# A fused patch embedding, top-k attention and routed FFN on one core: GpSimd's, TensorE's and ScalarE's orders rewritten, three row counts moved from ScalarE to VectorE

## The chip, the cores and the metric

The kernel runs on one core of one Trainium2 chip, as one program. The metric is the device time of an execution in microseconds; three executions of the kernel before gave 3077.92 (median), 3074.23 and 3079.49. An execution that the hardware profiler recorded took 3077.82 us, of which 3076.1 us are the span from the first to the last instruction.

## The reference

For 64 batches, 36 image patches and a class token are embedded (a 768 to 256 projection and a layer norm), and 128 text tokens are put behind them: T = 165 tokens of width 256. Then, in float32:

```
h = h + attention(layernorm(h))     # 16 heads of width 16; of each row of 165 scores
                                    # only the largest int(165*0.3) = 49 are kept
h = h + moe(layernorm(h))           # 64 experts of width 192, top 8 per token, capacity 128,
                                    # and one shared expert
```

Attention is `softmax` over the 49 kept scores of each row times `v`, and an output projection. There are 16*165 = 2640 score rows in a batch.

## The kernel before, in words

The work falls into two phases. In the first one, a loop over the batches (`batches`, unrolled, 68 iterations) does everything but the routed experts; in the second one, `experts` gathers rows for each expert. The change touches the first only.

One batch passes through several iterations, so that iteration i works on five of them at once. For batch i+1 it makes the front: norm, transposition, q, k and v (`front_*`) and the first score tiles. For batch i it makes scores and exponentials, and counts. For batch i-1 it selects the 49 values and masks. For batch i-2 it transposes the probabilities and multiplies by v (`transposes`, `transposed`, `values`), and projects. For batch i-3 it does the second norm, the shared expert and the routing (`back_*`). For batch i-4 GpSimd writes token numbers into a table in HBM by indirect DMAs (`back_slots` for text, 8 per batch; `packed` for image tokens, 8 per three batches: three in each of two iterations and two in the third). Every third iteration also embeds the patches of three batches (`trio(i+4)`: `front_embed*` on VectorE, `front_scale` and `front_affine` on GpSimd).

The 2640 rows are 21 tiles of 128 rows, in 7 groups of 3 tiles. TensorE makes a group's scores in one of three PSUM banks (`scores`), VectorE copies them to S and takes the row minima `nb` (`take`, L1083), ScalarE makes exponentials E and their sums `sz` (`exps`, L865). Selection searches a threshold per row. GpSimd guesses it from `nb` and `sz` (`guess`, half 0 is tiles 0 to 8, half 1 is tiles 9 to 20). ScalarE counts the values above the guess (`count` with n = 0, L877), GpSimd corrects it (`refine`), ScalarE counts again (n = 1), GpSimd corrects once more (`refine2`). GpSimd then writes X = (S + threshold) * 2^-40, a group at a time, into five rotating buffers (`apart`, L662). A third count is taken of X: by ScalarE for groups 0, 1, 2 (`third_count`, L890) and by VectorE for groups 3 to 6 (L1096). From it VectorE knows how far the count is off 49 and to which side (`side`, `side2`, for sets of groups: {0,1,2}, {3,4}, {5,6}), flips the signs by a bitwise xor (`one_side`, L1148), lists the eight nearest values (`nearest`, L1158, which frees the X buffer), ranks, and masks E into PR (`mask`, L1277).

Each engine runs its list `iteration(i, r)` strictly in the order in which it is written, and waits on semaphores that others raise. No planner or cost stands behind the order: it is written out by hand. GpSimd raises `s_up` 20 times per batch, and the waits name positions in that sequence. S and E have two buffers each, PTT and PTI (the transposed probabilities) one. ScalarE's copy of v into VZ (`front_v`, L853) and its copies of transposed quads (`transposed`, L901 to L906) free the PSUM banks for TensorE's next step. On the way back, GpSimd's `back_scale` (L651, L653) gives the norm's factor `brs` to VectorE's `back_norm`; TensorE transposes (L1757), ScalarE copies (X2T, L917), TensorE makes both halves of the shared expert (`back_glu`, L1766), ScalarE takes tanh (L921), and VectorE goes on (`back_glu`, L1320).

Of the kernel before, what the change touches and what calls it, by code (L numbers as in the profile page):

```python
# [60 lines left out]
RING = 4  # L61
# [9 lines left out]
def early_fusion_kernel(nc, patches, txt, w_tok, b_tok, cls, pos, gamma, beta, w_qkv, b_q, b_k, b_v, w_out, b_out,  # L71
# [3 lines left out]
    with ctx:  # L75
# [184 lines left out]
        THIRD = [3, 4, 5, 6]  # L260
# [3 lines left out]
        SETS = [(0, 1, 2), (3, 4), (5, 6)]  # L264
# [238 lines left out]
        def _(pool):  # L503
# [107 lines left out]
            def guess(i, r, half):  # L611

                lo, hi = HALVES[half]
                n = UP * i + 5 * half
                pool.wait_ge(s_exp, EX_N * i + hi)
                gated()
                pool.tensor_scalar(v0[:, lo:hi], nb[:, lo:hi], -GUESS[3], GUESS[1], ALU.mult, ALU.add).then_inc(s_up, 1)
                pool.tensor_scalar(v1[:, lo:hi], nb[:, lo:hi], -GUESS[2], GUESS[0], ALU.mult, ALU.add).then_inc(s_up, 1)
                pool.wait_ge(s_up, n + 1)
# [6 lines left out]
            def refine(i, r, half):  # L626
# [6 lines left out]
                pool.wait_ge(s_up, UP * i + 11 + 2 * half)  # L633
# [53 lines left out]
            def pack_tokens(n):  # L687
                if n >= 2:
                    pool.wait_ge(s_packed[n % 2], PS * (n // 2))
# [28 lines left out]
            def iteration(i, r):  # L718
# [8 lines left out]
                if has(i - 1):  # L727
                    apart(i - 1, (r - 1) % RING, 2)
                    apart(i - 1, (r - 1) % RING, 3)
                    apart(i - 1, (r - 1) % RING, 4)  # L730
                if has(i + 1):
                    front_bias(i + 1, (r + 1) % RING)
                if has(i):
                    guess(i, r, 0)
                if has(i - 1):
                    apart(i - 1, (r - 1) % RING, 5)
                if trio(i + 4):
                    front_scale((i + 4) // PACKED)
                if has(i - 1):
                    apart(i - 1, (r - 1) % RING, 6)  # L740
                if has(i - 4):
                    back_tokens(i - 4, r)
                if True:
                    packed(i, 0)
                    packed(i, 1)
                if has(i - 4):
                    back_slots(i - 4, r, 0, 2)
                if True:
                    packed(i, 2)
                if has(i):  # L750
                    guess(i, r, 1)
                if has(i - 4):
                    back_slots(i - 4, r, 2, 4)
                if has(i + 1):
                    front_center(i + 1)
                if has(i):
                    refine(i, r, 0)
                if has(i - 4):
                    back_slots(i - 4, r, 4, 6)
                if has(i):  # L760
                    refine(i, r, 1)
                if has(i - 4):
                    back_slots(i - 4, r, 6, 8)
                if trio(i + 4):
                    front_affine((i + 4) // PACKED)
                if has(i):
                    refine2(i, r, 0)
# [49 lines left out]
        def _(act):  # L817
# [38 lines left out]
            def exps(i, r, g):  # L856

                if g == 0:

                    ahead(act, s_up, UP * (i - 1) + 10, i - 1 if known(i) else i)  # L860
# [7 lines left out]
            def count(i, r, n, tiles):  # L868

                for t in tiles:  # L870
                    if t in (0, AHEAD):
                        half = t // AHEAD
                        act.wait_ge(s_up, UP * i + (5 + 5 * half, 12 + 2 * half)[n])
# [1067 lines left out]
```

## Time and profile before

| | us |
|---|---|
| three executions: median, lowest, highest | 3077.92, 3074.23, 3079.49 |
| the profiled execution, its span | 3077.82, 3076.1 |
| busy: TensorE matmuls, VectorE, ScalarE, GpSimd | 2360.4, 2486.5, 2480.2, 2181.0 |
| granted TensorE clock, mean over the span | 0.88 |

Busy is the time in which an engine ran an instruction other than register, branch, semaphore and DMA-issuing ones. The span holds both phases, so the share of busy time over all of it is lower than in the loop: in the last 350 us the engines other than TensorE do little. Rows of a timeline give the start (us from the span's start), how long the row took, the engine, the line of the kernel, the operation, what it writes and reads, and how many instructions are merged; in brackets the idle time before them, and what ended it.

### The profile page before, as it was taken

What the parts mean: (1) busy time and instruction counts of PE and PEld (TensorE: products, weight loads), DVE (VectorE), ACT (ScalarE), POOL (GpSimd) and SP (SyncE); (2) the same over time, 40 slices, a digit from 0 to 9 for tenths busy, and PEclk for the clock granted to TensorE, in tenths of its full rate; (3) what the DMA queues carried; (4) which work ended last, traced back from release to release, by engine and by line L of the source; (5) the groups of instructions that cost most, each with busy time, mean ns of one, the idle gap of its engine ahead of it and who ended that gap; (6) DMA issues with size and microseconds to landing.
All of it is one profiled execution on the core that took longest, in us unless ns stands there. A gap on an engine that the chain in (4) does not pass through costs nothing.

```text
span 3076.1 us, 74618 instructions
## 1 busy us (share of the span) xinstructions
PE 2360.4 (77%) x17233; PEld 2007.1 (65%) x17233; DVE 2486.5 (81%) x12929; ACT 2480.2 (81%) x11201; POOL 2181.0 (71%) x4319
## 2 busy tenths in 40 slices
PE   5677877778787778777887787787878787764887
PEld 4566666666676666666666676676667676544776
DVE  1798889888888899988989888988899888842444
ACT  3999999999999999989999899998999989811111
POOL 3457777777777777777777777777777777645665
PEclk7799988988999989988899889988888889867998
DMA  2011011010110110101101101001010100006886
GB/s 66 10 30 24 25 27 29 25 30 23 28 25 23 29 30 25 30 23 24 27 25 29 30 25 27 25 22 28 25 30 23 29 18 24 19 16 159 220 222 143
DMA packets 203389, 130.07 MB, mean 42 GB/s; under 512 B 101776, under 2 KB 194444, under 8 KB 202924
## 3 DMA queue, kind: packets, MB, share of 16 engines
q1 hardware_dynamic: 168064, 105.38, 12.7%
q0 software_dynamic: 34368, 19.34, 3.9%
q14 instruction: 333, 2.73, 0.3%
q8 instruction: 132, 2.16, 0.3%
q10 hardware_dynamic: 492, 0.45, 0.1%
HBM read 77.63 MB, written 34.09 MB: 36 GB/s over the span
## 4 chain that ended last, share of the span: by engine, by line
ACT 47%; PE 14%; POOL 13%; issue 11%; DVE 6%; DMA 4%; another core or an unknown queue 2%; ACTq 0%; POOLq 0%; SPq 0%; DVEq 0%
ACT JK L877 23%; ACT E L865 9%; PE bank L1766 4%; ACT PTT L901 4%; DMA out<-E,X 3%; ACT JL L890 3%; POOL slot_token L683 3%; ACT PTI L906 2%; PE bank L1688 2%; PE bank L1691 2%; POOL X L662 2%; POOL out L793 2%; ACT KT L843 1%; PE bank L1757 1%
## 5 line engine op out<-in xcount | busy, mean ns | idle before, releaser
L877 ACT ACTIVATE JK<-S,thr 128x165 f32<-128x165 f32 x2688 | 1120.5, 422 | 14.5 <-POOL thr L624 7.2
L683 POOL DMA_INDIRECT slot_token<-TOKI,SLOT x512 | 533.5, 1042 | 221.8 <-issue 204.4
L662 POOL TENSOR_SCALAR X<-S,nt 128x165 f32<-128x165 f32 x1344 | 582.7, 452 | 75.4 <-DVE LIST L1158 66.1
L865 ACT ACTIVATE E<-bank,nb 128x165 f32<-128x165 f32 x1344 | 508.5, 391 | 10.8 <-DVE S L1083 9.6
L877 ACT ACTIVATION_READ_ACCUMULATOR JK<-S,thr 128x1 f32 x2688 | 510.7, 190 | 0.0
L1277 DVE SCALAR_TENSOR_TENSOR PR<-S,TV,E 128x165 f32<-128x165 f32 x1344 | 480.1, 405 | 0.2
L1083 DVE TENSOR_SCALAR_CACHE_REDUCE S<-bank 128x165 f32<-128x165 f32 x1344 | 364.5, 320 | 86.9 <-PE bank L1691 47.4
L1705 PE MATMUL bank<-IDENT,PR 128*128 128x128 f32 x1344 | 222.2, 283 | 230.3 <-issue 116.1
L1158 DVE MAX8 LIST<-X 128x8 f32<-128x165 f32 x1344 | 351.3, 317 | 8.1 <-DVE X L1148 1.8
L1705 PEld LDWEIGHTS bank<-IDENT,PR 128*128 128x128 f32 x1344 | 154.8, 145 | 284.6 <-issue 163.2
L1688 PE MATMUL bank<-KZ,QA 128*128 128x165 f32 x1408 | 280.8, 346 | 45.6 <-ACT E L865 19.0
L1739 PE MATMUL bank<-PTT,VZ 128*32 128x165 f32 x2048 | 196.4, 432 | 149.9 <-ACT PTT L903 119.9
L1148 DVE TENSOR_TENSOR X<-X,flip 128x495 int32<-128x495 int32 x448 | 295.9, 662 | 0.0
L1688 PEld LDWEIGHTS bank<-KZ,QA 128*128 128x128 f32 x1408 | 231.6, 213 | 79.7 <-issue 73.0
L865 ACT ACTIVATION_READ_ACCUMULATOR E<-bank,nb 128x1 f32 x1344 | 271.7, 202 | 0.0
L1691 PE MATMUL bank<-KZ,QB 128*128 128x165 f32 x1408 | 267.9, 329 | 0.0
L706 POOL DMA_INDIRECT slot_token<-PACKI,PACK x176 | 193.9, 1102 | 81.2 <-issue 64.1
L890 ACT ACTIVATE JL<-X,tiny 128x165 f32<-128x165 f32 x576 | 241.2, 429 | 1.9 <-POOL X L662 1.9
L1691 PEld LDWEIGHTS bank<-KZ,QB 128*128 128x128 f32 x1408 | 233.8, 211 | 0.0
L1739 PEld LDWEIGHTS bank<-PTT,VZ 128*32 128x32 f32 x2048 | 98.3, 151 | 186.3 <-ACT PTT L903 134.7
L1096 DVE TENSOR_SCALAR_CACHE_REDUCE JD<-X 128x165 f32<-128x165 f32 x768 | 205.9, 316 | 3.2 <-issue 1.6
L1766 PE MATMUL bank<-X2T,WSG 128*96 128x165 f32 x1024 | 207.1, 370 | 1.6 <-ACT X2T L917 1.6
(211 smaller groups left out, 6358.3 us busy)
## 6 DMA issues: line engine op xcount, KB each, us to landing
S<-in_w_gate SPq DMA_DIRECT2D x64, 192.0 KB
S<-in_w_up SPq DMA_DIRECT2D x64, 192.0 KB
E<-in_w_down SPq DMA_DIRECT2D x64, 192.0 KB
RD<-inverses SPq DMA_DIRECT2D x128, 82.5 KB
x_rows<-X SPq DMA_DIRECT2D x64, 160.0 KB
H<-in_txt SPq DMA_DIRECT2D x64, 128.0 KB
QA<-QT SPq DMA_DIRECT2D x512, 10.3 KB
QB<-QT SPq DMA_DIRECT2D x512, 10.3 KB
```

What stands on the lines that cost most here:

```text
L662: last = pool.tensor_scalar(X[n % DEEP][:, t % GROUP, :], S[r % 2][:, t, :], nt[r % 2][:, t:t + 1], DOWN, ALU.add, ALU.mult)
L683: pool.indirect_dma_start(slot_token, bass.IndirectOffsetOnAxis(SLOT[r % 2][:, 0, k:k + 1], 0), TOKI[r % 2][:, :], None, bounds_check=SLOT ...
L865: act.activation(E[r % 2][:, t, :], chunks(bS[g % 3], GROUP, T)[:, t % GROUP, :], ACT.Exp, bias=nb[:, t:t + 1], scale=-1.0, accum_out=sz[: ...
L877: act.activation(JK[:, t % 4, :], S[r % 2][:, t, :], ACT.Sign, bias=(t0, t1)[n][:, t:t + 1], scale=-1.0, accum_out=(c0, c1)[n][:, t:t + 1] ...
L890: act.activation(JL[:, n % 3, :], X[(NG * i + g) % DEEP][:, k, :], ACT.Sign, bias=tiny[:, :], scale=-1.0, accum_out=c2[:, t:t + 1]).then_i ...
L1083: dve.tensor_scalar(S[r % 2][:, t, :], chunks(bS[g % 3], GROUP, T)[:, t % GROUP, :], 1.0, None, ALU.mult, ALU.min, accum_out=nb[:, t:t + 1 ...
L1158: dve.max(LIST[:, 0, WIN * t:WIN * t + WIN], X[n % DEEP][:, t % GROUP, :]).then_inc(s_list, 1)
L1277: dve.scalar_tensor_tensor(PR[:, t, :], S[r % 2][:, t, :], TV[:, t:t + 1], E[r % 2][:, t, :], ALU.is_le, ALU.mult, accum_out=den[:, t:t + ...
L1688: last = pe.matmul(o, QA[:, P * t:P * t + P], KZ[:, 0, :], start=True, stop=(t < MIXED))
L1691: last = pe.matmul(o, QB[:, at:at + P], KZ[:, 1, :], start=(t > MIXED), stop=True)
L1705: pe.transpose(bT[:, P * k:P * k + P], PR[:, t, IMG:T], IDENT[:, :])
L1766: last = pe.matmul(chunks(bank, NF, T)[0:FC, f, :], WSG[:, k, at:at + FC], X2T[:, k, :], start=(k == 0), stop=(k == KC - 1))
```

## The change

GpSimd: `guess` is cut in two. Its first two operations, which need `nb` only, wait for `take` (`s_take`); the three that need the exponentials' sums stay behind the wait for ScalarE (`guess2`). The order of the list is new: `front_scale` of a trio goes up between `apart` 2 and 3, `packed(i, 0)` goes ahead of `apart` 5, `front_affine` goes up behind `apart` 6, `front_center` and `refine` of half 0 go ahead of the guess of half 1, and fewer indirect DMAs stand ahead of that guess, more behind it; `refine2` of half 0 goes ahead of the last two. ScalarE: the third count of group 2 is gone, and `front_v` stands ahead of `transposed` 4. VectorE: group 2 is in `THIRD`, the sets are {0,1}, {2,3,4}, {5,6}, `take` 3 goes behind the shared expert and `front_norm2`, and `front_embed2` goes up. TensorE: `back_glu` goes ahead of `scores` 3, `front_v` ahead of `transposes` 4.

```diff
-        THIRD = [3, 4, 5, 6]
+        THIRD = [2, 3, 4, 5, 6]
-        SETS = [(0, 1, 2), (3, 4), (5, 6)]
+        SETS = [(0, 1), (2, 3, 4), (5, 6)]
...
             def guess(i, r, half):
                 lo, hi = HALVES[half]
-                n = UP * i + 5 * half
-                pool.wait_ge(s_exp, EX_N * i + hi)
+                pool.wait_ge(s_take, NT * i + hi)
                 gated()
                 pool.tensor_scalar(v0[:, lo:hi], ...)
                 pool.tensor_scalar(v1[:, lo:hi], ...)
+
+            def guess2(i, r, half):
+                lo, hi = HALVES[half]
+                n = UP * i + 7 * half
+                pool.wait_ge(s_exp, EX_N * i + hi)
+                gated()
                 pool.wait_ge(s_up, n + 1)
...
# GpSimd's iteration(i, r)
+                if trio(i + 4):
+                    front_scale((i + 4) // PACKED)
                     apart(i - 1, (r - 1) % RING, 3)
                     apart(i - 1, (r - 1) % RING, 4)
...
                     guess(i, r, 0)
+                    guess2(i, r, 0)
+                if True:
+                    packed(i, 0)
                 if has(i - 1):
                     apart(i - 1, (r - 1) % RING, 5)
+                    apart(i - 1, (r - 1) % RING, 6)
                 if trio(i + 4):
-                    front_scale((i + 4) // PACKED)
-                if has(i - 1):
-                    apart(i - 1, (r - 1) % RING, 6)
+                    front_affine((i + 4) // PACKED)
                 if has(i - 4):
                     back_tokens(i - 4, r)
                 if True:
-                    packed(i, 0)
                     packed(i, 1)
+                    packed(i, 2)
                 if has(i - 4):
-                    back_slots(i - 4, r, 0, 2)
-                if True:
-                    packed(i, 2)
-                if has(i):
-                    guess(i, r, 1)
-                if has(i - 4):
-                    back_slots(i - 4, r, 2, 4)
+                    back_slots(i - 4, r, 0, 1)
                 if has(i + 1):
                     front_center(i + 1)
                 if has(i):
                     refine(i, r, 0)
+                    guess(i, r, 1)
+                    guess2(i, r, 1)
+                if has(i - 4):
+                    back_slots(i - 4, r, 1, 4)
+                if has(i):
+                    refine(i, r, 1)
                 if has(i - 4):
                     back_slots(i - 4, r, 4, 6)
                 if has(i):
-                    refine(i, r, 1)
+                    refine2(i, r, 0)
                 if has(i - 4):
                     back_slots(i - 4, r, 6, 8)
-                if trio(i + 4):
-                    front_affine((i + 4) // PACKED)
-                if has(i):
-                    refine2(i, r, 0)
...
# ScalarE's
                     third_count(i - 1, 1)
-                    third_count(i - 1, 2)
...
-                    transposed(i - 2, 4)
                     front_v(i + 1, (r + 1) % RING)
+                    transposed(i - 2, 4)
                     transposed(i - 2, 5)
...
# VectorE's
-                    take(i, r, 3)
                     back_glu(i - 3)
                     back_glu2(i - 3)
                     front_norm2(i + 1, (r + 1) % RING)
+                    take(i, r, 3)
                     take(i, r, 4)
+                    third_count(i - 1, 2)
                     third_count(i - 1, 3)
                     side(i - 1, 0)
+                    front_embed2((i + 4) // PACKED)      # was behind threshold(i - 1)
...
# TensorE's
                     back_xt(i - 3, (r - 3) % RING)
+                    back_glu(i - 3)
                     scores(i, 3)
-                    back_glu(i - 3)
                     scores(i, 4)
...
-                    transposes(i - 2, 4)
                     front_v(i + 1)
+                    transposes(i - 2, 4)
                     transposes(i - 2, 5)
```

The numbers in waits on `s_up` are moved along with the new order, and `packed` waits for the emptied table at its first use, where `back_tokens` alone did.

## Rows read from the trace of the kernel before

**Rows 1.** The page: busy time of each engine, and the chain that ended last, by engine.
```profile
PE 2360.4 (77%) x17233; PEld 2007.1 (65%) x17233; DVE 2486.5 (81%) x12929; ACT 2480.2 (81%) x11201; POOL 2181.0 (71%) x4319
ACT 47%; PE 14%; POOL 13%; issue 11%; DVE 6%; DMA 4%; another core or an unknown queue 2%; ACTq 0%; POOLq 0%; SPq 0%; DVEq 0%
```

**Rows 2.** VectorE's reciprocal L1286, one per batch: duration, first and last start.
```profile
L1286 DVE RECIPROCAL inv<-den x64: 283/285/291, 118.6 to 2722.1; 128x21 f32<-128x21 f32 x64
```

**Rows 3.** Windows, one iteration each: length, busy time of the engines, clock, DMA.
```profile
979.50:1022.10 42.60, 32.03 (x252) 26.36 (x251) 39.05 (x200) 38.95 (x180) 34.00 (x72) 0.92 0.14 30
1022.10:1061.50 39.40, 30.95 (x241) 25.96 (x241) 36.16 (x196) 37.42 (x172) 29.60 (x63) 0.96 0.10 26
1061.50:1102.50 41.00, 33.14 (x245) 28.65 (x245) 35.98 (x196) 37.23 (x171) 31.48 (x67) 0.88 0.09 24
```

**Rows 4.** Waits of ScalarE and VectorE, 1000 to 2000 us: total, times, longest.
```profile
ACT VZ L853 <- remote: 35.1, 16, 2.7
ACT TH L921 <- PE bank L1766: 24.2, 16, 1.9
ACT X2T L917 <- PE bank L1757: 13.0, 15, 2.2
...
DVE TH L1320 <- ACT TH L921: 29.1, 21, 1.8
DVE X L1313 <- POOL brs L653: 21.0, 18, 3.5
DVE CT L1291 <- PE bank L1739: 13.5, 14, 1.6
```

**Rows 5.** Timelines around ScalarE's copy of v, in two iterations.
```profile
962.20 0.64 PE L1667 MATMUL bank<-WQ,XT 128*37 128x128 f32 x8
965.98 0.82 ACT L853 ACTIVATE VZ<-bank 128x256 f32<-128x256 f32 x3 [2.25 <-remote]
...
1047.38 0.81 ACT L853 ACTIVATE VZ<-bank 128x256 f32<-128x256 f32 x3
```

**Rows 6.** Timelines of a third count on ScalarE and one on VectorE.
```profile
984.77 0.44 ACT L890 ACTIVATE JL<-X,tiny 128x165 f32<-128x165 f32 x1
985.19 0.44 ACT L890 ACTIVATE JL<-X,tiny 128x165 f32<-128x165 f32 x1
...
989.05 0.31 DVE L1096 TENSOR_SCALAR_CACHE_REDUCE JD<-X 128x165 f32<-128x165 f32 x1
989.29 0.31 DVE L1096 TENSOR_SCALAR_CACHE_REDUCE JD<-X 128x165 f32<-128x165 f32 x1
```

**Rows 7.** Timeline of GpSimd: last threshold's start, an indirect DMA, the guess's end, centring, correction.
```profile
981.85 0.20 POOL L641 TENSOR_SCALAR cnt<-cnt 128x12 f32<-128x12 f32 x1
1002.27 0.99 POOL L683 DMA_INDIRECT slot_token<-TOKI,SLOT  x1 [0.30 <-issue]
1007.18 0.21 POOL L624 TENSOR_TENSOR thr<-cnt,nb 128x12 f32<-128x12 f32 x1
...
968.81 0.23 POOL L604 TENSOR_SCALAR ks<-ks 128x2 f32<-128x2 f32 x1
970.66 0.21 POOL L634 TENSOR_TENSOR thr<-thr,cnt 128x9 f32<-128x9 f32 x1
```

**Rows 8.** GpSimd's L578 in all executions: count, duration min, median, max.
```profile
L578 POOL TENSOR_TENSOR TK<-TK,GAM x22: 722/837/895, 23.6 to 2513.8; 111x256 f32<-111x256 f32 x22
```

**Rows 9.** Timeline of ScalarE: the first of 33 counts, and the exponential behind them.
```profile
967.37 0.43 ACT L877 ACTIVATE JK<-S,thr 128x165 f32<-128x165 f32 x1
981.30 0.38 ACT L865 ACTIVATE E<-bank,nb 128x165 f32<-128x165 f32 x1
```

**Rows 10.** Waits of GpSimd, 1000 to 2000 us.
```profile
POOL X L662 <- DVE LIST L1158: 20.0, 33, 1.7
```

**Rows 11.** Timeline: GpSimd's L622 beside VectorE's xor.
```profile
991.85 0.66 DVE L1148 TENSOR_TENSOR X<-X,flip 128x495 int32<-128x495 int32 x1
992.00 0.57 POOL L622 TENSOR_TENSOR cnt<-cnt 128x9 f32<-128x9 f32 x1
```

More of the change, by code:

```diff
@@ L632, in refine @@
                                    ALU.mult, ALU.add).then_inc(s_up, 1)
-                pool.wait_ge(s_up, UP * i + 11 + 2 * half)
+                pool.wait_ge(s_up, UP * i + (6, 13)[half])
                 pool.tensor_tensor(t1[:, lo:hi], t0[:, lo:hi], u0[:, lo:hi], ALU.mult).then_inc(s_up, 1)
@@ L687, in pack_tokens @@
             def pack_tokens(n):
+                if n == 0:
+                    pool.wait_ge(s_empty, 16)
                 if n >= 2:
@@ L728, in iteration @@
                     apart(i - 1, (r - 1) % RING, 2)
+                if trio(i + 4):
+                    front_scale((i + 4) // PACKED)
+                if has(i - 1):
                     apart(i - 1, (r - 1) % RING, 3)
@@ L858, in exps @@
                 if g == 0:
-                    ahead(act, s_up, UP * (i - 1) + 10, i - 1 if known(i) else i)
+                    ahead(act, s_up, UP * (i - 1) + 12, i - 1 if known(i) else i)
                     ahead(act, s_prob, NT * (i - 1), i - 2 if known(i) else i)
@@ L872, in count @@
                         half = t // AHEAD
-                        act.wait_ge(s_up, UP * i + (5 + 5 * half, 12 + 2 * half)[n])
+                        act.wait_ge(s_up, UP * i + (5 + 7 * half, 7 + 7 * half)[n])
                     if t % 2 == 0 and (n or t or not known(i) or i):
@@ L976, in iteration @@
                     exps(i, r, 6)
-                if has(i - 2):
-                    transposed(i - 2, 4)
                 if has(i + 1):
@@ L1076, in take @@
                     ahead(dve, s_exp, EX_N * i, i - 1)
-                    ahead(dve, s_up, UP * (i - 1) + 10, i - 1 if known(i) else i)
+                    ahead(dve, s_up, UP * (i - 1) + 12, i - 1 if known(i) else i)
                     ahead(dve, s_xp, NG * (i - 1), i - 2)
@@ L1420, in iteration @@
                     front_embed_aggr((i + 4) // PACKED)
-                if has(i):
-                    take(i, r, 3)
                 if has(i - 3):
@@ L1428, in iteration @@
                 if has(i):
+                    take(i, r, 3)
                     take(i, r, 4)
                 if has(i - 1):
+                    third_count(i - 1, 2)
                     third_count(i - 1, 3)
                     side(i - 1, 0)
+                if trio(i + 4):
+                    front_embed2((i + 4) // PACKED)
                 if has(i - 3):
@@ L1497, in iteration @@
                     threshold(i - 1)
-                if trio(i + 4):
-                    front_embed2((i + 4) // PACKED)
                 if has(i - 1):
@@ L1807, in iteration @@
                     back_xt(i - 3, (r - 3) % RING)
-                if has(i):
-                    scores(i, 3)
                 if has(i - 3):
@@ L1812, in iteration @@
                 if has(i):
+                    scores(i, 3)
                     scores(i, 4)
@@ L1836, in iteration @@
                     front_qk(i + 1, 1)
-                if has(i - 2):
-                    transposes(i - 2, 4)
                 if has(i + 1):
```

## The prediction

> **What bounds the kernel now.** I read the page first: over the span VectorE and ScalarE are busy for the same 81%, GpSimd for 71%, and the chain that ended last is ScalarE's for 47% of its length [rows 1]. The span holds the quiet expert phase, so I turned to the loop. VectorE's reciprocal comes once per batch: (2722.1 - 118.6) / 63 = 41.33 us per iteration [rows 2]. Three iterations cut at that instruction show a pattern of three: 42.6 us (the one that embeds patches), 39.4 and 41.0 [rows 3]. In them ScalarE is busy for 38.95, 37.42 and 37.23 us and VectorE for 39.05, 36.16 and 35.98. No engine is full: ScalarE stands 2.0 to 3.8 us per iteration, VectorE 3.2 to 5.0. The bound is a ring of ordered lists that wait for one another, and ScalarE has the least slack.
>
> So the waits count. Between 1000 and 2000 us (24.2 iterations) ScalarE waits 35.1 us before its copy of v, 24.2 before the tanh and 13.0 before X2T; VectorE waits 29.1 us for the tanh, 21.0 for `brs` and 13.5 for `values` [rows 4]. Per iteration these are 1.45, 1.00, 0.54, 1.20, 0.87 and 0.56 us. The largest is odd: the last matmul of `front_v` ends at 962.84 by the trace, and ScalarE, free for it after `transposed` 4, copies at 965.98 after 2.25 us of idling. It happens in two of three iterations; in the third there is no wait (1047.38) [rows 5], and that is the iteration of 39.4 us with two packed DMAs in place of three. The wait is thus worth about what separates 41.0 from 39.4, and it comes with GpSimd's DMA burst, though no row says how.
>
> **The change, part by part.** *Third counts of tiles 6 to 8.* ScalarE issues one every 985.19 - 984.77 = 0.42 us, VectorE one every 989.29 - 989.05 = 0.24 [rows 6]. Three leave ScalarE: -1.26 us. Three come to VectorE: +0.73. They need X of group 2, which GpSimd has ready before group 3, whose count stands next on VectorE now without a wait: no wait is added. With the sets regrouped, the sides of groups 0 and 1 need ScalarE's first two counts only, which are earlier; group 2's side then waits for group 4's count on VectorE itself. I take 0 for this, with bounds of -0.3 (earlier `nearest`, so earlier X buffers; GpSimd waits 20.0 / 24.2 = 0.83 us for them [rows 10]) and +0.3.
>
> *`back_glu` ahead of `scores` 3 on TensorE.* It takes away the wait that made ScalarE idle before the tanh: -1.00 [rows 4], and scores 3 come a `back_glu` later, which `take` 3, now behind the shared expert on VectorE, does not need earlier. But that `take`, about 0.75 us, no longer fills VectorE's wait for the tanh. VectorE gets the tanh 1.00 earlier and arrives 0.75 earlier: its wait stays near 1.2; I take 1.4, with bounds 0.4 and 2.0.
>
> *`front_v` ahead of the fourth transposes, on both engines.* Without the stall the copy runs as soon as the exponentials are done, but the copy of quad 4, TensorE's quad 5 and its copy are now one after the other with nothing between: +0.8 us on ScalarE (the 0.82 us of VZ copies used to cover them [rows 5]). If the 2.25 us goes in two iterations of three, it gives 1.5 per iteration; if it stays, ScalarE loses 0.8. Bounds for both together: -1.45 to +0.8; I take -0.3, since one of the five DMAs ahead of that place leaves it and the burst comes earlier, but nothing in the rows excludes a new burst on it.
>
> *GpSimd's order.* This is the part that can cost. From the start of the last `refine2` (981.85) to the end of the second guess (1007.39) it needs 25.54 us in the embedding iteration [rows 7]. In the new list one indirect DMA fewer lies between (each 0.99 with 0.30 ahead: -1.3), and the 0.83 us wait for X is filled by `packed(i, 0)` (-0.8); `front_center` and `refine` of half 0 come in between (968.81 to 970.87: +2.06 [rows 7]), and in the embedding iteration `front_affine` too (two operations of 0.84: +1.67 [rows 8]). That makes 27.2 us there and, with neither `front_affine` nor the 1.1 us of `front_scale`, 24.4 in the two others. Behind the guess ScalarE has 33 counts until it starts the next exponentials: 981.30 - 967.37 = 13.93 us [rows 9]. So the ring of the two engines is 41.2 us in the embedding iteration and 38.4 in the others, 39.3 in the mean, against 42.6, 39.4 and 41.0 now. Two DMAs now stand between the first `refine2` and `back_scale`: up to 2.6 us later `brs` if GpSimd is late; it has the 13.93 us to do some 13.5 us of work (seven DMAs at 1.3 and 4.4 of corrections, their gaps and the scale), so it just fits. I leave VectorE 0.5 us of its 0.87 us wait for `brs`, with bounds of 0 and 2.0. The two guess operations that run earlier save nothing where GpSimd arrives after the exponentials, up to 0.5 us where it waits for them. `front_affine` comes some 15 us earlier, and `front_embed2` with it: the load of the image rows is off the path, at most 0.3 us in one iteration of three.
>
> *Sum.* ScalarE: 37.87 busy (mean of the three) - 1.26 = 36.6, well below VectorE. VectorE: (39.05 + 36.16 + 35.98) / 3 = 37.06 busy [rows 3], + 0.73 = 37.8, + waits of 1.4 (tanh), 0.5 (`brs`) and 0.3 (small ones; the wait for `values` goes, as these start a stall earlier) = 40.0 us. This is above GpSimd's ring of 39.3, so VectorE becomes the bound, and the gain is 41.33 - 40.0 = 1.3 us. Over the 61 iterations in which all stages are full: 79 us. The profiled execution took 3077.8, the median of the runs is 3077.9, so both give 2999; the expert phase is not touched.
>
> One rule speaks against moving counts to VectorE. Beside VectorE's xor of two inputs from SBUF (0.66 us at 991.85) GpSimd's 9-column L622 took 0.57 [rows 11], where its neighbours take 0.21. The Trainium skill (GPSIMD Engine Reference, 1. Specifications) says that GpSimd shares its interfaces to SBUF with VectorE and contends with instructions that have two SBUF inputs. By that rule the trace agrees for the xor, and the three added counts, with one SBUF input, would hold GpSimd up by nothing; if they did hold it, 0.73 us per iteration would go onto GpSimd's ring, 39.3 to 40.0, still no longer than VectorE's.
>
> **The rivals.** *A, the stall goes altogether.* For it: the iteration without it runs at 39.4 with ScalarE at 37.4 busy. VectorE's waits would shrink as well, to 0.8 (tanh), 0.3 (`brs`) and 0.3: 37.8 + 1.4 = 39.2 us, 2.1 less than now, 2948. Against it: `front_v` still lies beside indirect DMAs. *B, GpSimd takes it back.* Its list becomes the ring: `brs` comes 1.4 us late (2.6 of DMAs less the slack), VectorE stands at 37.8 + 1.4 + 1.4 + 0.3 = 40.9 to 41.3: 3051 to 3077, say 3062. For it: GpSimd's 34.0 us busy in the embedding iteration, and gaps ahead of DMAs on top. *C, the stall stays and TensorE's new order adds to it.* ScalarE then gains 1.26 + 1.0 - 0.8, but VectorE pays its 0.73 and waits for `values` as before: 40.7 us, 3040. *D, slower.* Place: ScalarE's count of half 1, which waits for the second guess, in all iterations. Price: the guess comes behind centring, correction and, every third time, `front_affine`. If the four DMAs ahead take 1.6 us in place of 1.3 (+1.2) and a stall like that of `front_v` comes on top (+1.5), the ring is 25.3 (the mean of 27.2, 24.4 and 24.4) + 2.7 + 13.93 = 41.9 us in the mean: 3077.8 + 61 * 0.6 = 3114. It decides from about 2 us of added lateness of that guess, 41.33 - 39.3. Against it: by the sum above the ring is 1.0 to 2.6 us shorter than each of the three iterations now. That the change does not do what it says can be excluded only for the counts; the stall's cause isn't shown, so C covers it.
>
> **How the numbers follow.** Forecast 0.40 (2999, its own range 2975 to 3025), A 0.16, C 0.14, B 0.16, D 0.14. About 0.2%, or 6 us, is what a measurement of this kernel can tell from no change. B holds 0.06 of "within 0.2%" and 0.01 of slower; D holds 0.01 of "within": faster 0.79, same 0.07, slower 0.14. The range 2942 to 3085 takes in A and B and leaves out most of D and the far end of A.
>
> **What would show it.** VectorE's reciprocals 40.0 us apart; in the pattern of three, the two non-embedding iterations alike at 39 to 39.5 and the embedding one near 41.2; ScalarE's wait for the tanh gone; the wait before VZ below 1 us per iteration; 576 - 192 = 384 counts L890 left; ScalarE's share below VectorE's in the loop. Wrong if ScalarE waits for GpSimd's guess for more than 1 us per iteration (D), if VectorE waits for `brs` for more than 1.4 (B), or if the wait before VZ is still 1.45 (C).

## The result, and the profile after

The changed kernel takes 3196.09 us (median of four, 3193.91 to 3203.36) against 3077.56 for the kernel before on the same chip: a ratio of 1.039, with an interval of 1.0371 to 1.041. The forecast was 2999, faster. The profiled execution took 3203.36 us, its span is 3201.5.

First the page of the changed kernel, as in [rows 1], then its reciprocal L1293, which answers to [rows 2].

```profile
PE 2450.0 (77%) x17233; PEld 2045.5 (64%) x17233; DVE 2506.5 (78%) x13313; ACT 2412.3 (75%) x10817; POOL 2216.8 (69%) x4319
...
PE 27%; ACT 21%; issue 17%; POOL 15%; DVE 14%; DMA 4%; POOLq 1%; ACTq 0%; SPq 0%; another core or an unknown queue 0%; DVEq 0%
```

```profile
L1293 DVE RECIPROCAL inv<-den x64: 283/284/292, 120.3 to 2845.0; 128x21 f32<-128x21 f32 x64
```

The loop takes (2845.0 - 120.3) / 63 = 43.25 us per iteration, 1.92 more than before, and 63 times that, 121 us, is the whole loss. ScalarE's part of the chain fell from 47% to 21%. TensorE has the same 17233 matmuls and is busy for 90 us more. Three iterations of the changed kernel, cut at that instruction (length, busy time of PE, PEld, DVE, ACT, POOL, granted clock, DMA), answer to [rows 3]:

```profile
1155.54:1198.48 42.94, 32.95 (x252) 26.48 (x251) 38.30 (x206) 37.27 (x170) 33.77 (x68) 0.96 0.12 27
1198.48:1241.17 42.69, 33.75 (x244) 27.83 (x242) 36.60 (x202) 36.34 (x166) 30.06 (x63) 0.88 0.11 26
1241.17:1285.29 44.12, 36.55 (x244) 30.95 (x244) 36.67 (x204) 37.41 (x172) 31.69 (x66) 0.81 0.08 22
```

The embedding iteration, the first, is hardly longer than before; the two others are 42.7 and 44.1 us where they were 39.4 and 41.0. In the third TensorE needs 36.55 us at a granted clock of 0.81. The waits between 1000 and 2000 us (23.1 iterations), for [rows 4] and [rows 10]:

```profile
ACT XT L838 <- PE bank L1733: 68.8, 23, 4.0
ACT X2T L926 <- PE bank L1764: 24.7, 23, 3.3
...
ACT VZ L862 <- PE bank L1674: 6.0, 11, 0.9
ACT TH L930 <- PE bank L1773: 4.2, 18, 0.2
ACT JK L886 <- POOL thr L630: 2.6, 7, 0.7
...
DVE X L1320 <- POOL brs L659: 40.3, 23, 3.9
DVE TH L1327 <- ACT TH L930: 35.6, 23, 2.1
DVE CT L1298 <- PE bank L1746: 27.7, 22, 2.1
DVE HT L1333 <- PE bank L1773: 20.8, 18, 1.3
...
POOL X L668 <- DVE LIST L1165: 32.2, 41, 2.0
```

The two waits that the change took from ScalarE are nearly gone: VZ from 35.1 to 6.0, tanh from 24.2 to 4.2. A larger one stands in their place: 3.0 us of each iteration for the transposed `XT`, which comes behind `back_glu` on TensorE. (The row names L1733, a small transposition right behind that of XT, for which this copy waits too.) VectorE waits for `brs` twice as long as before, and for HT three times as long (6.8 us before). GpSimd waits longer for its X buffers, 32.2 us where it was 20.0.

Now TensorE's timeline (start, duration, what was idle before it) at the second norm, and windows: in the changed kernel those of the wait, of the transposition and of `back_glu`, in the kernel before that of `back_glu` alone. First the changed kernel, then the kernel before as it ran in e8.

```profile
1200.78 1.05 PE L1764 MATMUL bank<-IDENT,X 128*128 128x128 f32 x4 [2.02 <-DVE X L1320]
1202.37 4.66 PE L1773 MATMUL bank<-X2T,WSG 128*96 128x165 f32 x16 [0.54 <-ACT X2T L926]
1206.86 0.72 PE L1695 MATMUL bank<-KZ,QA 128*128 128x165 f32 x4
...
1211.11 0.29 PE L1733 MATMUL bank<-IDENT,inv 128*21 128x128 f32 x1
...
1198.76:1200.78 2.02, 0.01 (x1) 0.00 (x0) 0.80 (x4) 2.02 (x11) 1.59 (x6) 0.81 0.32 52
1200.78:1201.83 1.05, 1.05 (x4) 0.57 (x4) 1.04 (x7) 0.21 (x2) 1.05 (x4) 0.50 0.04 9
1202.37:1206.86 4.49, 4.49 (x17) 4.49 (x17) 1.46 (x9) 4.26 (x19) 4.23 (x12) 0.50 0.00 0
```

```profile
1219.96 0.62 PE L1757 MATMUL bank<-IDENT,X 128*128 128x128 f32 x4
1220.51 0.83 PE L1688 MATMUL bank<-KZ,QA 128*128 128x165 f32 x4
1221.18 0.72 PE L1691 MATMUL bank<-KZ,QB 128*128 128x165 f32 x4
1221.74 2.41 PE L1766 MATMUL bank<-X2T,WSG 128*96 128x165 f32 x16
...
1221.74:1223.99 2.25, 2.25 (x19) 2.25 (x17) 1.49 (x11) 2.25 (x11) 2.07 (x6) 1.00 0.00 0
```

In the kernel before the score matmuls of `scores` 3 run while ScalarE copies X2T, and `back_glu` follows without a gap. In the changed kernel TensorE waits 2.02 us for the norm, works for 1.05, waits 0.54, and the sixteen matmuls take 4.66 us at a granted clock of 0.50 (1.2 GHz) where they took 2.41 at 1.00 (2.4 GHz). The clock fell in the wait for the norm already (0.81 in it, 0.50 in the transposition behind it), so it was low before the missing scores could matter; what the order decides is which work meets the low clock. In the mean of the iterations between 1000 and 2000 us a matmul of `back_glu` takes 440 ns, 356 before. The page "TensorE: Matmul & The Clock Gate" of the Trainium skill (HAM oscillation — how this bites in real kernels) tells of a loop whose wait for a DMA comes back in each pass, so that the clock falls and is paid for in each. By that the trace agrees, with waits for other engines in place of DMAs: in the 1000 us the transposition waits for the norm 23 times, 50.4 us in all.

The same at `front_v`, with the window from the end of `front_qk` to `values` behind each. Changed kernel, then before as in e8, where the fourth transposes, L1705 to L1715, stand between `front_qk` and `front_v`:

```profile
1219.56 1.29 PE L1664 MATMUL bank<-XT,WQ 128*128 128x165 f32 x8
1223.03 1.26 PE L1671 MATMUL bank<-WQ,XT 128*128 128x256 f32 x4 [2.19 <-ACT KT L852]
...
1225.24 1.12 PE L1712 MATMUL bank<-IDENT,PR 128*128 128x128 f32 x4
...
1227.90 0.34 PE L1712 MATMUL bank<-IDENT,PR 128*128 128x128 f32 x1 [0.69 <-ACT PTT L910]
...
1229.25 0.49 PE L1746 MATMUL bank<-PTT,VZ 128*32 128x165 f32 x8 [0.79 <-ACT PTT L912]
...
1220.85:1229.25 8.40, 4.74 (x24) 3.12 (x24) 8.33 (x39) 6.56 (x28) 5.78 (x12) 0.80 0.18 52
```

```profile
1194.41 1.29 PE L1657 MATMUL bank<-XT,WQ 128*128 128x165 f32 x8
1197.11 0.63 PE L1705 MATMUL bank<-IDENT,PR 128*128 128x128 f32 x4 [1.41 <-ACT PTT L901]
...
1198.01 1.03 PE L1664 MATMUL bank<-WQ,XT 128*128 128x256 f32 x4
...
1200.57 0.33 PE L1705 MATMUL bank<-IDENT,PR 128*128 128x128 f32 x1 [0.95 <-DVE N L1381]
...
1202.00 0.49 PE L1739 MATMUL bank<-PTT,VZ 128*32 128x165 f32 x8 [0.89 <-ACT PTT L903]
...
1195.70:1202.00 6.30, 3.05 (x23) 2.20 (x24) 6.30 (x32) 6.17 (x26) 5.08 (x5) 1.00 0.17 40
```

From the end of `front_qk` to `values`: 1229.25 - 1220.85 = 8.4 us against 1202.00 - 1195.70 = 6.3. TensorE waits in both, 3.7 us in three waits against 3.3 in three (2.19, 0.69, 0.79; 1.41, 0.95, 0.89). The greater part of the 2.1 us is the work itself: 4.74 us at a mean granted clock of 0.80 against 3.05 at 1.00.

### The profile page after: what moved, and what is told of

It reads as the page before. It is cut to its first block, busy times and chain, and to the rows that moved or that the text cites. A ratio compares the mean times of both kernels' runs of the same rounds, so it can differ in the third digit from the quotient of the medians.

```text
span 3201.5 us, 74746 instructions
## 1 busy us (share of the span) xinstructions
PE 2450.0 (77%) x17233; PEld 2045.5 (64%) x17233; DVE 2506.5 (78%) x13313; ACT 2412.3 (75%) x10817; POOL 2216.8 (69%) x4319
## 4 chain that ended last, share of the span: by engine, by line
PE 27%; ACT 21%; issue 17%; POOL 15%; DVE 14%; DMA 4%; POOLq 1%; ACTq 0%; SPq 0%; another core or an unknown queue 0%; DVEq 0%
ACT JK L886 11%; PE bank L1773 7%; POOL slot_token L689 5%; PE bank L1746 4%; DMA out<-E,X 3%; ACT E L874 3%; ACT PTT L910 2%; DVE JD L1103 2%; DVE PR L1284 2%; PE bank L1712 2%; PE bank L1698 2%; PE bank L1671 2%; POOL out L802 2%; DVE S L1090 2%; PE bank L1782 2%
## 5 line engine op out<-in xcount | busy, mean ns | idle before, releaser
L1284 DVE SCALAR_TENSOR_TENSOR PR<-S,TV,E 128x165 f32<-128x165 f32 x1344 | 450.3, 384 | 0.0
L1712 PE MATMUL bank<-IDENT,PR 128*128 128x128 f32 x1344 | 248.3, 307 | 118.6 <-ACT PTT L910 56.5
L1773 PE MATMUL bank<-X2T,WSG 128*96 128x165 f32 x1024 | 262.5, 439 | 37.7 <-ACT X2T L926 37.7
L1773 PEld LDWEIGHTS bank<-X2T,WSG 128*96 128x96 f32 x1024 | 239.5, 250 | 46.1 <-ACT X2T L926 46.1
L1695 PE MATMUL bank<-KZ,QA 128*128 128x165 f32 x1408 | 254.1, 323 | 17.8 <-ACT E L874 16.1
L1103 DVE TENSOR_SCALAR_CACHE_REDUCE JD<-X 128x165 f32<-128x165 f32 x960 | 253.6, 317 | 1.0 <-POOL X L668 0.7
L1746 PE MATMUL bank<-PTI,VZ 128*32 128x165 f32 x2048 | 205.8, 363 | 43.3 <-issue 42.1
L1698 PE MATMUL bank<-KZ,QB 128*128 128x165 f32 x1408 | 235.0, 309 | 0.0
L910 ACT ACTIVATE PTT<-bank 128x512 f32<-128x512 f32 x320 | 187.3, 585 | 53.3 <-PE bank L1722 51.1
L1746 PE MATMUL bank<-PTT,VZ 128*32 128x165 f32 x2048 | 171.7, 366 | 59.9 <-ACT PTT L912 40.5
## 6 DMA issues: line engine op xcount, KB each, us to landing
QA<-QT SPq DMA_DIRECT2D x512, 10.3 KB
QB<-QT SPq DMA_DIRECT2D x512, 10.3 KB
```

The lines of the kernel that those rows point to most:

```text
L1103: dve.tensor_scalar(JD[:, n % 3, :], X[(NG * i + g) % DEEP][:, k, :], 0.0, None, ALU.is_lt, ALU.add, accum_out=c2[:, t:t + 1]).then_inc(s_ ...
L1284: dve.scalar_tensor_tensor(PR[:, t, :], S[r % 2][:, t, :], TV[:, t:t + 1], E[r % 2][:, t, :], ALU.is_le, ALU.mult, accum_out=den[:, t:t + ...
L1695: last = pe.matmul(o, QA[:, P * t:P * t + P], KZ[:, 0, :], start=True, stop=(t < MIXED))
L1712: pe.transpose(bT[:, P * k:P * k + P], PR[:, t, IMG:T], IDENT[:, :])
L1746: last = pe.matmul(o[2 * HD * g:2 * HD * (g + 1)], VZ[r][:, c, 2 * HD * h:2 * HD * (h + 1)], p, start=(n == 0), stop=(n == 3), skip_group_ ...
L1773: last = pe.matmul(chunks(bank, NF, T)[0:FC, f, :], WSG[:, k, at:at + FC], X2T[:, k, :], start=(k == 0), stop=(k == KC - 1))
```

## The experiments

Theory 1: the ring runs through the second norm. `brs` comes late behind two indirect DMAs, TensorE idles, and `back_glu` runs at the low clock. Theory 2: the new order of TensorE costs by itself, through XT. They are so numbered in e5 to e7 and e15; e1 and e2 give them the opposite numbers, and e10, e11, e13 and e14 name theories of their own. Each run is compared with the kernel before on its own chip. The kernel before took 3027.55 beside e1 to e4, 3036.55 beside e5 to e7, 3037.25 beside e9 to e12, 3032.45 beside e13 to e16, and 3074.94 beside e17 and e18. The table gathers what the traces show, in us per iteration: the loop (reciprocal to reciprocal), and the means between 1000 and 2000 us of three stretches of TensorE: V, from the end of `front_qk` to the start of `values`; N, from the second norm's transposition to the end of L1733, right behind XT's; P, from the end of the projection to that transposition.

| run | what it is | ratio, interval | loop | V | N | P |
|---|---|---|---|---|---|---|
| before | (first chip) | 1 | 41.33 | 8.0 | 9.3 | 6.7 |
| e8 | before, again | 3031.97 us, one run | 40.78 | 6.4 | 8.6 | 6.4 |
| after | (first chip) | 1.039, 1.0371 to 1.041 | 43.25 | 8.2 | 10.1 | 7.3 |
| e9 | after, again | 1.0505, 1.0428 to 1.0581 | 43.30 | 8.3 | 10.4 | 8.5 |
| e4 | before + third counts | 1.0103, 1.0055 to 1.0151 | 41.32 | 6.2 | 8.7 | 6.1 |
| e7 | before + GpSimd's order | 1.017, 1.0131 to 1.0209 | 41.48 | 6.2 | 8.5 | 7.0 |
| e3 | before + `front_v` ahead | 1.0257, 1.0213 to 1.0301 | 42.12 | 8.4 | 10.3 | 7.1 |
| e2 | before + `back_glu` ahead on PE | 1.0391, 1.0345 to 1.0436 | 42.61 | 6.4 | 10.8 | 6.3 |
| e14 | after, third counts back | 1.0458, 1.0404 to 1.0512 | 43.21 | 8.3 | 10.5 | 8.6 |
| e15 | after, GpSimd's order back | 1.0371, 1.0319 to 1.0423 | 42.55 | 8.1 | 10.5 | 7.0 |
| e13 | after, `front_v` back | 1.0276, 1.0224 to 1.0327 | 42.17 | 6.4 | 9.7 | 7.2 |
| e6 | after, `back_glu` and `take` 3 back | 1.0346, 1.0307 to 1.0386 | 42.28 | 8.0 | 9.4 | 8.4 |
| e1 | after, `back_glu` back on PE only | 1.0675, 1.0604 to 1.0746 | 43.90 | 8.1 | 10.3 | 8.7 |
| e5 | after, `back_scale` first | 1.0312, 1.0275 to 1.0348 | 42.34 | 7.9 | 12.0 | 5.6 |
| e10 | e6 with e5 | 1.0278, 1.0202 to 1.0354 | 42.11 | 7.5 | 11.2 | 5.6 |
| e11 | e10 with `front_v` back | 1.021, 1.0135 to 1.0286 | 41.96 | 6.0 | 10.1 | 5.6 |
| e12 | before + guess early | 1.0052, 1.0022 to 1.0083 | 41.21 | 6.4 | 9.0 | 6.3 |
| e16, e18 | before + `front_center` early | 0.9974, 0.9947 to 1.0; 0.9976, 0.996 to 0.9991 | 41.05, 41.12 | 6.4, 8.0 | 9.0, 9.3 | 6.9, 6.1 |
| e17 | e18 with `back_scale` early | 1.0192, 1.0166 to 1.0218 | 42.24 | 7.9 | 11.1 | 5.6 |

**e1, e2: `back_glu` and `scores` 3 on TensorE, alone.** e1 takes this part of the change back, e2 puts it into the kernel before.

```diff
+                    back_glu(i - 3)
                     scores(i, 3)
-                    back_glu(i - 3)
                     scores(i, 4)
```

> The changed kernel with TensorE's list put back at one place: back_glu behind scores 3. Theory 1 (TensorE: back_glu right behind back_xt runs at the lower clock, 4.7 us in place of 2.4, and pushes scores 3 and 4, back_down and front_xt, for which ScalarE waits 3 us per iteration): most of the loss comes back, 3090 to 3130 us, the wait before XT under 1 us per iteration. Theory 2 (GpSimd: two DMAs ahead of back_scale make brs late, 1.75 us per iteration, and TensorE idles for it): little comes back, 3165 to 3200 us, the wait before XT only falls by the 2.3 us of the clock and moves to the tanh.

> The kernel before with this one edit: TensorE's back_glu ahead of scores 3 (VectorE's take 3 stays ahead of its back_glu). Theory 1: slower by itself, 3130 to 3190 us, back_glu's matmuls longer and ScalarE waiting before XT. Theory 2: within 15 us of before, since brs is no later.

e2 is 3.9% slower, and its trace shows XT's wait at 61.8 us in 23 times (0.2 in e8). But VectorE's `take` 3 stayed ahead of the shared expert there and now waits 81.1 us for its scores, so e2 bounds the move from above. Its matmuls of `back_glu` take 405 ns (333 in e8) although `brs` is no later there (14.6 us, 15.8 in e8). Its time, 3149.26, lies in the range of the theory on TensorE; that of e1, 3235.00, lies above both. e1 has the opposite mismatch (VectorE's list wants the tanh first, TensorE gives the scores first: VectorE's wait for the tanh goes from 35.6 to 73.4 us) and is slower still. Neither isolates the move; e6 does.

**e3, e4, e7: the other parts, alone in the kernel before**, as their hunks stand in the diff above; e8 is the kernel before itself on e7's chip.

> The kernel before with front_v ahead of the fourth transposes on TensorE and ScalarE, nothing else. The prediction's step: -0.3 us per iteration (bounds -1.45 to +0.8), so 3060 us (2990 to 3127). If the wait of 2.25 us before the copy of v belongs to TensorE's order there, it goes and the gain is 1 us or more per iteration: 3015 or less. If it belongs to GpSimd's burst of DMAs, it stays, and the kernel is slower: 3090 to 3127.

> The kernel before with only the third counts of group 2 moved from ScalarE to VectorE and the sets regrouped. The prediction's step: ScalarE -1.26, VectorE +0.73 us per iteration, so faster by 0.4 to 1.2 us per iteration if ScalarE sets the pace: 3003 to 3053. If TensorE's late halves of the shared expert and brs set it, the 1.26 us turn into a longer wait before the tanh and VectorE's 0.73 is added: 3077 to 3120.

> The kernel before with GpSimd's new list (guess in two, the new order of the indirect DMAs, centring, corrections, front_affine) and front_embed2 moved up; TensorE, ScalarE and the third counts as before. Theory 1: slower by itself by 1.5 to 3%, VectorE's wait for brs over 1.5 us per iteration. Theory 2: within 1% of before.

> The kernel before itself, to have its trace from the chip of these runs. If its lower time on another chip (3028 us) comes from the late signal of front_v, its wait before VZ is shorter here than 1.45 us per iteration; if it comes from all parts alike, the waits are the same.

None of the four parts is worth anything alone; they cost 1.0, 1.7, 2.6 and at most 3.9%, up to 9.2% together where the whole costs 5.05% (e9). That they share waits fits this, but is not shown. In e3 TensorE waits for KT, and stretch V goes from 6.4 to 8.4 us: 1.5 us of it are longer work (4.6 in place of 3.05) and 0.4 are waiting (3.8 in place of 3.4). In e7, GpSimd's order with VectorE's `front_embed2`, the ratio is in theory 1's range (1.5 to 3%), the wait for `brs` below its 1.5 us (32.8 / 24.1 = 1.4). The waits are the two that the prediction named, rival D's place and B's, and TensorE's for CT, which stands where e8 has 65.5 us for KZ:

```profile
PE bank L1757 <- DVE CT L1300: 62.5, 24, 3.9
...
ACT JK L886 <- POOL thr L630: 36.4, 24, 2.8
DVE X L1322 <- POOL brs L659: 32.8, 16, 3.4
```

The wait for the guess (L630) is 1.5 us per iteration against 24.4 / 24.5 = 1.0 in e8. e4 saves ScalarE 36 us of work between 1000 and 2000 us (889.98 busy, 926.19 in e8), yet is slower: ScalarE spends 29.0 of them waiting for XT. That time was not on the path.

**e5, e6: two sources of the late second norm, taken out of the changed kernel.**

```diff
# e5, GpSimd
+                    back_scale(i - 2)
                     back_slots(i - 4, r, 6, 8)
-                    back_scale(i - 2)
# e6: scores(i, 3) on TensorE and take(i, r, 3) on VectorE ahead of back_glu, as before
```

> The changed kernel with one move on GpSimd: back_scale ahead of the last two indirect DMAs, in place of behind them. Theory 1 (the ring that now ends last runs through brs: the statistics wait for two DMAs, 2.7 us, before the second norm can start, and TensorE idles and falls to the lower clock for the shared expert): brs comes about 2.5 us earlier, VectorE's wait for it of 1.75 us per iteration nearly goes, and the kernel gains 1.5 to 2.5 us per iteration against the changed one: within 1% of before. Theory 2 (TensorE's order alone costs it, through front_xt): gain under 0.5 us per iteration, still 3% above before, the wait before XT stays at 3 us.

> The changed kernel with back_glu behind scores 3 on TensorE and take 3 ahead of back_glu on VectorE again, both as before; GpSimd's order, front_v and the third counts stay changed. Theory 2: the loss from TensorE's order goes, 0 to 1.5% above before. Theory 1: brs is still late, so it stays 2 to 4% above before, with a wait for brs of 1.7 us or more per iteration.

In e5 the wait for `brs` goes from 40.3 us to 0.8, and the ratio is 1.0312 where the whole has 1.0505 (e9, another chip). Part of what was gained is handed on: with the norm earlier, X2T waits its turn behind ScalarE's counts and three exponentials, VectorE's wait for the tanh doubles, and XT is as late as before. Theory 1 (within 1% of the kernel before) is missed; the ratio and XT's wait are theory 2's, but the 0.9 us gained in the loop is more than its 0.5.

```profile
DVE TH L1327 <- ACT TH L930: 74.6, 24, 4.6
ACT XT L838 <- PE bank L1733: 73.1, 24, 4.1
...
PE bank L1773 <- ACT X2T L926: 55.8, 24, 2.9
```

In e6 `back_glu` takes 357 ns a matmul again (440 in the changed kernel, 356 before) and XT's wait is 30.8 us in place of 68.8. `brs` is later than in the changed kernel (64.8 us), and the clock is down at the norm no less: the transposition of X, L1765, takes 347 ns a matmul, 331 in the changed kernel and 308 before.

```profile
L1774 PE MATMUL bank<-X2T,WSG 128*96 128x165 f32 x384 | 73.9, 357 | 0.0
L1765 PE MATMUL bank<-IDENT,X 128*128 128x128 f32 (+1 forms) x96 | 22.5, 347 | 77.4 <-DVE X L1320 77.4
```

So the scores run in the time of the copy, and `back_glu` comes behind them, mostly at a higher clock; this brings 1.6% back. The ratio of 3.46% lies in theory 1's range (2 to 4%, with `brs` late): the order of `back_glu` is a part of the loss, not the greater one.

**e9 to e11: the changed kernel again, and the repairs together.**

> The changed kernel as it is, once more, beside the kernel before on one chip: the yardstick for the three runs beside it. If the ratio belongs to the two programs, it is the 1.037 to 1.041 of the first comparison again. If part of it belonged to the chip of that comparison (where TensorE's end of front_v reached ScalarE 2.7 to 3.6 us late in the kernel before, a stall that the other chip did not show), it is above 1.041 here, since the kernel before then has less to lose there: 1.045 to 1.055.

> The changed kernel with scores 3 and take 3 ahead of back_glu as before, and GpSimd's back_scale ahead of its last two DMAs. Theory 1 (the ring: with scores 3 back in front of back_glu the second norm still waited 2.7 us of each iteration for brs, which came behind two DMAs): the wait for brs goes below 0.3 us of each iteration and the loop falls from about 42.3 to 41.0 us, a ratio of 1.010 to 1.018. Theory 2 (front_v behind the copy of KT, 2.0 us of each iteration on TensorE, is the next bound): brs comes in time, but TensorE's wait for KT stays and the ratio is 1.022 to 1.030, hardly below the 1.031 of back_scale alone.

> The same with front_v back between the fourth and the fifth transposes on both engines; what is left of the change is the third counts on VectorE and GpSimd's new order with back_scale ahead of its last two DMAs. Theory 1 (the two parts left cost 1.0% and up to 1.7% on their own): 1.010 to 1.020, about the same as the run beside it. Theory 2 (front_v ahead was what held the rest): 1.000 to 1.008 and at least 0.8% below the run beside it, with no wait of TensorE for KT behind front_v.

e9 gives 3190.87 us, as on the first chip, but the kernel before takes 3037.25 here: the ratio belongs in part to the chip (below). In e10 the wait for `brs` is gone (0.4 us) and XT's is half of what it was (35.2), and the ratio is 1.0278, within theory 2's range: TensorE's wait for KT (46.3 us) stayed, as that theory said. In e11 it is gone too, and another 0.7% (the two intervals overlap), far from the 1.000 to 1.008 of theory 2 and just above the 1.010 to 1.020 of theory 1. What is left, the third counts and GpSimd's order, cost 1.0 and 1.7% on their own. In e11's trace ScalarE waits 35.1 us for the guess, 1.5 per iteration, and 30.9 for XT.

**e13 to e15: one part out of the whole.** Undone are, in turn, `front_v` on both engines, the third counts with their sets, and GpSimd's list with the guess and VectorE's `front_embed2`.

> The changed kernel with front_v back between the fourth and the fifth transposes on both engines. Theory 1 (back_glu at the low clock, behind a late second norm, sets the loop; front_v's wait for KT lies in what the ring has to spare): 1.043 to 1.052, as the whole change beside the kernel before. Theory 2 (TensorE's 2.1 us for KT of each iteration are on the path): 1.025 to 1.035.

> The changed kernel with the counts of tiles 6 to 8 back on ScalarE. ScalarE has idle time in the changed kernel (3.0 us of each iteration before it copies XT), VectorE's three counts stand ahead of the side's mask. Theory 1 (they are a part of the delay on VectorE): 0.7 us an iteration less, 1.030 to 1.040. Theory 2 (they are hidden beside TensorE's waits): 1.045 to 1.055.

> The changed kernel with GpSimd's list and the guess as before (and the embed's second step late again); the three other parts stay. Theory 1 (brs behind two DMAs, 1.8 to 2.9 us late in each iteration, is a main part of the loss): the wait falls below 1 us and the ratio to 1.030 to 1.038. Theory 2 (the order of TensorE alone does it, front_xt and XT): XT's wait stays at 3 us of each iteration and the ratio at 1.045 to 1.055.

`front_v` back is worth the most: from 1.0505 to 1.0276, and 1.13 us of the loop (e9 to e13). Stretch V is 6.4 us again, with TensorE busy for 3.05 of them and waiting for 3.3 (4.6 and 3.7 in e9), and theory 1 of that run is refuted. GpSimd's order is worth 1.3%, though the wait for `brs` fell only to 31.1 / 23.5 = 1.3 us, not below theory 1's 1 us, and XT's stayed (66.9). The third counts are worth 0.5%, within the intervals: hidden. With `front_v` back, rival D's wait shows up in the whole as well:

```profile
ACT XT L838 <- PE bank L1734: 65.3, 24, 3.6
...
ACT JK L886 <- POOL thr L630: 31.6, 23, 2.4
```

**e12, e16 to e18: can the kernel before be made faster?** e12 issues the guess's two early operations ahead of the exponentials and puts half 1's guess ahead of the third packed DMA. e16 and e18 are one kernel; e17 adds a second move:

```diff
# e16 and e18, GpSimd
+                    front_center(i + 1)
                     back_slots(i - 4, r, 2, 4)
-                    front_center(i + 1)
# e17: also back_scale(i - 2) ahead of back_slots(i - 4, r, 6, 8),
#      front_affine and refine2(i, r, 0)
```

> The kernel before with one thing of the change: the guess's two operations that need only the bounds are issued ahead of the wait for the exponentials, and half 1's whole guess stands ahead of the third packed DMA. ScalarE's count of half 1 waits 1.0 us of each iteration for this guess in the kernel before. If that wait lies on the ring: it goes nearly altogether and the loop is 0.5 to 1.0 us shorter, a ratio of 0.975 to 0.990. If the ring runs elsewhere (brs, second norm, KZ): the wait goes and the time stays, 0.997 to 1.003; if the packed DMA behind the guess then delays brs by its 1.5 us, 1.005 to 1.015.

> The kernel before with front_center ahead of the two slot DMAs that it stands behind on GpSimd. TensorE waits 2.6 us of each iteration with the first scores of the next batch for KZ, which front_center makes; KT has been there for 8 us by then. If this wait holds the projection behind it and the second norm, KZ comes 2.6 us sooner and the loop is 0.8 to 1.5 us shorter: 0.965 to 0.980. If the projection's own operand comes no sooner than now (CT), the wait only moves: 0.995 to 1.003. If the two DMAs behind it delay the refining of the threshold and brs: 1.003 to 1.010.

> The kernel before with front_center ahead of two slot DMAs on GpSimd, and back_scale ahead of the last two slot DMAs, the embed's affine and the refining of half 0. The second norm waits 0.7 to 1.0 us of each iteration for brs in the kernel before and in e16. If that wait lies on the ring: it goes, and the ratio is 0.975 to 0.990. If the ring waits elsewhere (the threshold of half 0, now three operations later, or the projection for CT): 0.995 to 1.002.

> front_center alone once more, for a narrower interval beside e17: 0.997 with an interval of 0.995 to 1.000 if the first comparison holds, so that at most 0.1 us of each iteration came out of the 2.6 us that TensorE waited.

e12: ScalarE's wait for the guess falls from 24.4 to 7.7 us, and 23.4 us of waiting for the first correction (L640) come in its place: 0.5% slower. e16 takes TensorE's wait for KZ (L1688) from 65.5 us (e8) to 7.1, 2.4 per iteration, and a wait of 48.4 us for CT comes behind it (3.9 in e8). The ratio of 0.9974 is 0.13 us per iteration, a twentieth of what was waited; with the repetition, 0.9976, this version beats both kernels by a little. e17, outside both ranges that were expected, is the lesson on the other side of e5. `back_scale` now asks for the statistics before VectorE has them, and GpSimd, which runs in order, stands still with all that is behind it:

```profile
POOL bve L651 <- DVE bmv L1306: 74.7, 23, 4.1
```

This is 3.2 us in each iteration, spent to save a wait for `brs` of under 1 us, and the kernel is 1.9% slower.

## Why the prediction was wrong

*The reading of the loop* held: a ring of ordered lists with no engine full. But the sum was then made for VectorE by itself, 37.8 busy and 2.2 of waits. Between 1000 and 2000 us of the changed kernel VectorE is busy for 853.65 / 23.1 = 36.9 us per iteration, less than said, and idle for 6.3: tanh 1.5 (said: 1.4), `brs` 1.7 (0.5), `values` 1.2 (0), HT 0.9 (not named), and small ones. The waits that I added up are what the ring leaves over. They can't give its length.

*The third counts*: 384 of them left, and ScalarE's busy time is 846.87 / 23.1 = 36.6, just as said. Worth nothing: e4 is 1.0% slower.

*`back_glu` ahead of `scores` 3* is one of the two steps that failed. "It takes away the wait that made ScalarE idle before the tanh: -1.00": the wait went (1.00 to 0.18 us), and XT's came, 3.0 us per iteration. I wrote that `scores` 3 come later and that nobody needs them earlier. I did not ask what TensorE does while ScalarE copies X2T, and did not see that `front_xt` stands behind `back_glu`. The scores were the cover: they filled the copy's time and met the low clock that the wait for the norm leaves, and without them `back_glu` meets it (440 ns a matmul for 356). e6 prices it at 1.6% (1.0505 to 1.0346, across two chips).

*`front_v` ahead of the fourth transposes* is the other, and the larger: -0.3 us was taken, with bounds of -1.45 and +0.8, and e13 measures +1.1 in the loop. The +0.8 on ScalarE had the right place and was too small: the two waits for PTT, 1.06 and 0.65 us in that iteration, are 31.8 / 23.1 = 1.4 us in the mean, and the kernel before has 0.9 us of them in 1000. On TensorE nothing was counted. Its 2.2 us in one piece for KT were not seen, and the work behind them runs at the lower clock. Its waits between `front_qk` and `values` hardly grew in sum, from 3.4 us per iteration in e8 to 3.7 in e9; its work in that stretch grew from 3.05 to 4.6 us, at a mean granted clock of 0.80 for 1.00. No run separates the clock from the new order; with `front_v` back both are as before (e13). And the stall of 2.25 us that was to go did go, into a stretch of the same length: V is 8.0 us with the stall in the kernel before, and 8.2 without it in the changed one. Where the chip shows no stall the kernel before needs 6.4, and the change only costs.

*GpSimd's order*: "so it just fits" did not fit. `brs` waits 1.7 us per iteration on the first chip and 66.4 / 23.1 = 2.9 in e9. The timeline shows the scale behind two DMAs, the statistics having been ready at 1196.52:

```profile
1196.47 1.05 POOL L689 DMA_INDIRECT slot_token<-TOKI,SLOT  x1 [0.61 <-issue]
1197.83 1.00 POOL L689 DMA_INDIRECT slot_token<-TOKI,SLOT  x1 [0.30 <-issue]
1198.90 0.24 POOL L657 TENSOR_SCALAR bve<-bmv 128x2 f32<-128x2 f32 x1
```

This is B's mechanism, at B's size (1.4) or above it, but B took VectorE's other waits as given and so came out at 3062. D, the only rival on the right side, had 3114 and the wrong place: in the whole the count waits 2.6 us in all for the guess. Its wait is real, 1.5 and 1.3 us per iteration in e7 and e13 (1.0 in e8), and in the whole, with `front_v` ahead, it does not show.

What stays open: put into the kernel before one by one, the parts cost up to 9.2%, and the whole costs 5.05; taken out of the whole one by one they give 2.3, 1.6, 1.3 and 0.5%, and `back_scale` alone, moved ahead of two DMAs, gives 1.9, more than all of GpSimd's order. No run says why the third counts and GpSimd's order, left alone in e11 with `brs` in time, still cost 2.1%; the wait for the guess there is rival D's place, and no run takes it out of e11.

## What to carry to other kernels

Before an item is moved on an engine, ask what it covered where it stood: an item between a producer and its reader on another engine is often there to fill the copy's time. Here both swaps on TensorE removed such a filler, and the engine paid less for the wait than for the work behind it, which ran at a lower clock: of the 1.8 us by which the stretch around `front_v` grew from e8 to e9, 1.5 were longer matmuls. So compare busy time and granted clock stretch by stretch, not waits alone. And in a ring of ordered lists the time is not one engine's busy time plus its waits; follow one item round all engines through the new order, and write the new waits down, before a removed wait is counted as a gain.

## What the hardware did that was not expected

- The kernel before has two times: about 3076 us on the chips of the first comparison and of e17 and e18, and 3027 to 3037 on the others. The changed kernel took 3196 and 3191 on one of either kind. The traces of the slower kind all have the wait before VZ at the kernel before's place of `front_v` (first line: e18), and those of the other (e8, e16) don't have it; there TensorE waits for KZ instead (second line: e8).

```profile
ACT VZ L853 <- remote: 36.1, 16, 2.7
```

```profile
PE bank L1688 <- issue: 65.5, 25, 4.3
```

- The stall of 2.25 us in two iterations of three, 1.5 us per iteration, thus comes with some 42 us in 63 iterations, 0.7 per iteration. That it costs them, and not something else of those chips, was not tested. What delays TensorE's signal is not shown.
- TensorE can lose more by a lower clock behind a wait than by the wait: at `front_v` 1.5 us of work against 0.3 of waiting per iteration (e8 to e9), and 1.5 against 0.4 in e3.
- The same matmuls cost 2.0 us more of TensorE's time per iteration (794.27 / 23.1 against 783.88 / 24.2; e9 against e8, 1.6) after two swaps that added none.
